# Token blocks turned by four transposing transfers each in the expert stage

## The chip, the core and the metric

The kernel runs on one core of a Trainium2 chip. The core has five engines that work side by side: TensorE (PE: matrix products, with PEld for its weight loads), VectorE (DVE), ScalarE (ACT), GpSimd (POOL) and SyncE (SP, which here only issues DMAs). Each has its own queue of instructions, and they wait for each other on semaphores. Products go to PSUM, which VectorE and ScalarE read; tiles that TensorE reads lie in SBUF. The metric is the time of one execution on the device, in microseconds.

## The reference

One decoder layer on 2 x 1024 tokens of 256 numbers: self-attention with 16 heads, cross-attention with 16 heads over 77 context rows, and a mixture of 8 experts of which each token takes 2, each followed by a residual and a normalisation. The change lies in the experts:

```python
logits = jnp.einsum('bsd,de->bse', x, Wg) + bg
topk_vals, topk_idx = jax.lax.top_k(logits, TOP_K)
topk_w = jax.nn.softmax(topk_vals, axis=-1)
h = jax.nn.relu(jnp.einsum('bsd,edf->bsef', x, W1) + b1)
eo = jnp.einsum('bsef,efd->bsed', h, W2) + b2
sel = jnp.take_along_axis(eo, topk_idx[..., None], axis=2)
mixed = jnp.sum(sel * topk_w[..., None], axis=2)
y = mixed + x
```

## The kernel before

Self-attention fills the first two thirds of the time, cross-attention follows, and the expert stage runs from about 670 us to the end. It computes only the chosen experts. For each half h of the tokens POOL scatters every token's row twice, once for each chosen expert, into a table in memory, `xs[h]` (x_sorted), sorted by expert and padded so that each block of P = 128 rows belongs to one expert. A row has 512 bf16 numbers: 256 that hold the upper part of x and 256 that hold the rest (high and low part). There are HB = 23 blocks a half, BLOCKS = 46 in all. `tab` tells the expert of each block; each engine that needs the number reads it from SBUF into a register (`value_load`: L755 on TensorE, L1358 on ScalarE).

A block m goes through these steps:

- SyncE loads its 128 rows of 1 KB into `xb[:, m % 8]` (`load_block`, L379).
- TensorE turns them (`turn_block`, L748): four transposes of 128 x 128 into a PSUM bank, since the products need the 256 features on the partitions.
- ScalarE copies the bank to `xbT[:, m % 3]` (`keep_block`, L1353).
- TensorE makes the hidden layer (`hidden`, L767): 24 products of 128 x 128 x 128, transposed, with w1 of the expert.
- ScalarE adds the bias and takes the relu (`relu`, L1363, four instructions), VectorE splits the result into a high and a low part (L1036, L1038).
- TensorE makes the output (`output`, L783): 12 products with 256 columns. VectorE adds the bias (`keep_y`, L1049) into one of YB = 3 buffers, and SyncE stores it to `ys[h]` (`store_block`, L384).

When all blocks of a half are stored, POOL gathers two rows for each token (`gather`, L1544), 16 indirect DMAs a half, and VectorE mixes and normalises them. POOL's scatter is L1533, 16 indirect DMAs a half too; the second half's runs beside the first blocks, the first half's gather beside the blocks after the 23rd.

Nothing plans the order: it is the program order of each engine. TensorE's loop over m is turn(m + 3), hidden(m + 2), output(m), with turns 0 to 2 and hidden 0 and 1 ahead of the loop; so in its last three rounds nothing is turned. SyncE has LEAD = 6 loads ahead of the loop, then load(m + 6) and store(m) in each round; a load waits until TensorE has turned the block whose place it takes (`xb_turned`, XB = 8 places).

Of the kernel before, what the change touches and what calls it, by code (L numbers as in the profile page):

```python
# [6 lines left out]
ACT = mybir.ActivationFunctionType  # L7
AX_X = mybir.AxisListType.X
F32 = mybir.dt.float32
BF16 = mybir.dt.bfloat16  # L10
# [3 lines left out]
P = 128  # L14
B, S, D = 2, 1024, 256
# [3 lines left out]
NT = B * S // P  # L19
# [47 lines left out]
XB, YB = 8, 3  # L67
# [3 lines left out]
def build(nc, t):  # L71

    with ExitStack() as ctx:
        def sb(name, shape, dt=F32):
            return ctx.enter_context(nc.sbuf_tensor(name, shape, dt))

        def sem(name):
            return ctx.enter_context(nc.semaphore(name))

        bank = [ctx.enter_context(nc.psum_tensor(f"bank{i}", [P, 512], F32)) for i in range(4, 8)]  # L80
        quad = ctx.enter_context(nc.psum_tensor("quad", [P, 4, 512], F32))
        bank = [quad[:, i, :] for i in range(4)] + [b[:, :] for b in bank]
# [4 lines left out]
        xs = [nc.dram_tensor(f"x_sorted{h}", (XROWS, 2 * D), BF16, kind="Internal").ap() for h in range(2)]  # L87
# [4 lines left out]
        ident16 = sb("ident16", [P, P], BF16)  # L92
# [101 lines left out]
        logits = sb2("logits", [P, NT, NE])  # L194
        second.close()

        xb = sb("xb", [P, XB, 2 * D], BF16)
        xbT = sb("xbT", [P, 3, 4, P], BF16)
        hid = sb("hid", [P, 2, FC, P])
        hh = sb("hh", [P, 2, FC, P], BF16)  # L200
        hl = sb("hl", [P, 2, FC, P], BF16)
# [26 lines left out]
        s2_summed, s2_recip, p2_done, p2_turned, pT_done = map(sem, ("s2_summed", "s2_recip", "p2_done", "p2_turned", "pT_done"))  # L228
# [14 lines left out]
        xb_loaded = [sem(f"xb_loaded{i}") for i in range(XB)]  # L243
        xb_turned, xbT_done = sem("xb_turned"), sem("xbT_done")
        h_ready, hid_done, hh_done, hl_done = map(sem, ("h_ready", "hid_done", "hh_done", "hl_done"))
# [22 lines left out]
        BLOCKS = 2 * HB  # L268
# [10 lines left out]
        def _(sp):  # L279
# [93 lines left out]
            def load_block(m):  # L373
                h, i = m // HB, m % HB
                if i == 0:
                    sp.wait_ge(scattered[h], 16 * 2 * HT)
                if m >= XB:
                    sp.wait_ge(xb_turned, m - XB + 1)
                sp.dma_start(xb[:, m % XB, :], xs[h][i * P:(i + 1) * P, :]).then_inc(xb_loaded[m % XB], 16)  # L379

            def store_block(m):
                h, i = m // HB, m % HB
# [15 lines left out]
            for m in range(LEAD):  # L398
                load_block(m)
# [13 lines left out]
        def _(pe):  # L413
# [75 lines left out]
            for half in range(2):  # L489
                for c in range(C2):  # L490
                    mm = pe.matmul(bank[6][:, half * B * SC:(half + 1) * B * SC], w_in["cwk"][:, c, half * P:half * P + P], ctxT[:, c, :],
                                   start=(c == 0), stop=(c == C2 - 1))
            mm.then_inc(cross_ready, 1)
            for b in range(B):
                for c in range(C2):
                    mm = pe.matmul(bank[7][0:SC, b * D:(b + 1) * D], ctxT[:, c, b * SC:(b + 1) * SC], w_in["cwv"][:, c, :],
                                   start=(c == 0), stop=(c == C2 - 1))
# [94 lines left out]
            def turn_x2(g):  # L592

                pe.wait_ge(x2_done, g * 4 + 4)
                if g:
                    pe.wait_ge(x2T_done, g * 2)
                else:
                    pe.wait_ge(y2_done, 4 * (TG - 1))
                for c in range(C2):
                    for i in range(4):  # L600
                        tr = pe.transpose(bank[6 + c][:, i * P:i * P + P], xres[:, 4 * g + i, c * P:c * P + P], ident[:, :])
                    tr.then_inc(x2_turned, 1)

            def logits2(g):

                pe.wait_ge(x2T_done, 2 * g + 2)
                pe.wait_ge(s2_taken, NT)
                for i in range(4):
                    for c in range(C2):
                        mm = pe.matmul(LOGITS[g][:, i * NE:(i + 1) * NE], x2T[:, c, i * P:(i + 1) * P], wg[:, c, :],  # L610
                                       start=(c == 0), stop=(c == C2 - 1))
                mm.then_inc(logits_ready, 1)
# [99 lines left out]
            for n in range(NT):  # L712
                g, i = n // 4, n % 4
# [23 lines left out]
                    project_o2(g)  # L737


            def turn_block(m):  # L740

                pe.wait_ge(xb_loaded[m % XB], 16 * (m // XB) + 16)
                if m >= 2:
                    pe.wait_ge(xbT_done, m - 1)
                else:
                    pe.wait_ge(pT_done, 3 * NT)
                for c in range(4):
                    tr = pe.transpose(bank[4 + m % 2].bitcast(BF16)[:, c * P:(c + 1) * P], xb[:, m % XB, c * P:(c + 1) * P], ident16[:, :])  # L748
                tr.then_inc(xb_turned, 1)

            def hidden(m):

                h, i = m // HB, m % HB
                pe.wait_ge(tab_done, h + 1)
                e = pe.value_load(tab[0:1, h, i:i + 1], min_val=0, max_val=NE - 1)  # L755
                if m == 0:
                    pe.wait_ge(w_loaded_all, 32)
                    pe.wait_ge(s2_taken, NT)
                pe.wait_ge(xbT_done, m + 1)
                if m >= 3:  # L760
                    pe.wait_ge(hid_done, FC * (m - 2))
                else:
                    pe.wait_ge(logits_taken, m + 1)
                for fc in range(FC):
                    terms = [(half, part, c) for c in range(C2) for half, part in ((0, 0), (0, 1), (1, 0))]
                    for k, (half, part, c) in enumerate(terms):
                        mm = pe.matmul(bank[m % 3][:, fc * P:(fc + 1) * P], w1[:, bass.ds(e, 1), half, c, fc * P:(fc + 1) * P].rearrange("p o f -> p (o f)"),  # L767
                                       xbT[:, m % 3, 2 * part + c, :], start=(k == 0), stop=(k == len(terms) - 1))
                mm.then_inc(h_ready, 1)
                return e  # L770

            def output(m, e):

                pe.wait_ge(hl_done, m + 1)
                if m >= 2:
                    pe.wait_ge(y_done, m - 1)
                elif m == 1:
                    pe.wait_ge(x2T_done, C2 * TG)
                else:
                    pe.wait_ge(y2_done, NT)  # L780
                terms = [(a, half, fc) for fc in range(FC) for a, half in ((hh, 0), (hl, 0), (hh, 1))]
                for k, (a, half, fc) in enumerate(terms):
                    mm = pe.matmul(bank[Y_BANK[m % 2]][:, 0:D], a[:, m % 2, fc, :],  # L783
                                   w2[:, bass.ds(e, 1), half, fc, :].rearrange("p o d -> p (o d)"), start=(k == 0), stop=(k == len(terms) - 1))
                mm.then_inc(y_ready, 1)

            for m in range(3):
                turn_block(m)
            experts = [hidden(0), hidden(1)]
            for m in range(BLOCKS):  # L790
                if m + 3 < BLOCKS:
                    turn_block(m + 3)
                if m + 2 < BLOCKS:
                    experts.append(hidden(m + 2))
                output(m, experts.pop(0))
                if m == 0:
                    pe.wait_ge(y_done, 1)
                    turn_x2(TG - 1)
                    logits2(TG - 1)
                elif m == 1:  # L800
                    rank(2)
                elif m == 2:
                    rank(3)
# [409 lines left out]
        def _(act):  # L1213
# [122 lines left out]
            for n in range(NT):  # L1336
                g, i = n // 4, n % 4
# [8 lines left out]
                    exp2(n + FAR - 1)  # L1346


            def keep_block(m):
                act.wait_ge(xb_turned, m + 1)  # L1350
                if m >= 3:
                    act.wait_ge(h_ready, m - 2)
                act.activation(xbT[:, m % 3, :, :], bank[4 + m % 2].bitcast(BF16)[:, 0:4 * P].rearrange("p (c q) -> p c q", q=P), ACT.Copy).then_inc(xbT_done, 1)  # L1353

            def relu(m):
                h, i = m // HB, m % HB
                act.wait_ge(tab_done, h + 1)
                e = act.value_load(tab[0:1, h, i:i + 1], min_val=0, max_val=NE - 1)  # L1358
                if m >= 2:
                    act.wait_ge(hl_done, m - 1)  # L1360
                act.wait_ge(h_ready, m + 1)
                for fc in range(FC):
                    act.activation(hid[:, m % 2, fc, :], bank[m % 3][:, fc * P:(fc + 1) * P], ACT.Relu, bias=b1[:, bass.ds(e, 1), fc]).then_inc(hid_done, 1)  # L1363

            def exp_gap(h):
                act.wait_ge(gap_done, h + 1)
                act.activation(gw[:, HT * h:HT * h + HT, 1], gw[:, HT * h:HT * h + HT, 0], ACT.Exp).then_inc(gap_exp, 1)
# [4 lines left out]
                    act.activation(acc[:, n, :], acc[:, n, :], ACT.Identity, bias=lnv[:, 6, n:n + 1], scale=lnv[:, 2, n:n + 1]).then_inc(out_done, 1)  # L1372

            exp_gap(0)
            for m in range(3):
                keep_block(m)
            for m in range(BLOCKS):
                relu(m)
                if m == 1:
                    keep_x2(TG - 1)  # L1380
                if m + 3 < BLOCKS:
                    keep_block(m + 3)
                if m == 4:
                    exp_gap(1)
                for g in range(2):
                    if m == LAST[g]:
                        finish_tiles(g)
# [247 lines left out]
```

## Time and profile before

| what | us |
|---|---|
| median of 3 runs | 975.97 (975.21 to 976.09) |
| the profiled execution | 975.68 |
| its span, first to last instruction | 973.9 |
| TensorE busy in the span | 778.8 (80%) |
| VectorE busy | 622.5 (64%) |
| ScalarE busy | 458.0 (47%) |
| POOL busy | 304.3 (31%) |
| mean granted clock of TensorE | 0.905 of 2.4 GHz |

The median is what counts; the profile is one execution, and its times are from the span's start. An engine's busy time tells little by itself: what matters is the chain of waits, which is followed back from the last instruction to whatever released each step. "Issue" in it is time in which an engine waited for nothing that the profile shows. Busy matmuls overlap: one takes 0.2 us from start to end, but the next can start after 0.05 to 0.11 us, so their starts show the pace.

### The profile page before, as it was taken

The numbers are of one execution on the slowest core, as the hardware profiler recorded it, in microseconds if no ns is written. First come the engines' busy times: TensorE is split into PE (matmuls) and PEld (weight loads), VectorE is DVE, ScalarE is ACT, GpSimd is POOL, SyncE is SP. The second block draws the span as 40 slices with busy tenths as digits, with TensorE's granted clock in tenths as the row PEclk, the third lists the DMA queues.
The fourth block names the chain that finished last, engine by engine and source line by source line (L and its number), as shares of the span: only waits on it lengthen the run. The fifth ranks groups of instructions, "written<-read, shape, count | busy, mean of one in ns | idle before, by whom it ended". The sixth has DMA issues, their size and how long they took to land.

```text
span 973.9 us, 14837 instructions
## 1 busy us (share of the span) xinstructions
PE 778.8 (80%) x4736; PEld 384.1 (39%) x4736; DVE 622.5 (64%) x983; ACT 458.0 (47%) x919; POOL 304.3 (31%) x311
## 2 busy tenths in 40 slices
PE   6767999989999999999788887865485998599700
PEld 3433222222222222222235555562364776377600
DVE  3468787877888888888469889652242332286346
ACT  2112667767777777777654324330132443245300
POOL 6000086866000000000146566413323002355074
PEclk9978999999999999999999999957696999599955
DMA  7661529796405040400008000002222222322231
GB/s 223 158 174 52 143 97 273 265 260 220 88 1 88 2 87 2 87 1 1 0 1 345 1 0 1 1 0 91 78 77 87 67 66 83 92 66 62 88 87 43
DMA packets 53682, 86.64 MB, mean 89 GB/s; under 512 B 16425, under 2 KB 41257, under 8 KB 52457
## 3 DMA queue, kind: packets, MB, share of 16 engines
q1 hardware_dynamic: 41689, 53.25, 20.2%
q0 software_dynamic: 9280, 31.20, 9.7%
q10 hardware_dynamic: 2640, 1.24, 0.6%
q8 instruction: 43, 0.70, 0.3%
q14 instruction: 30, 0.25, 0.1%
HBM read 48.15 MB, written 33.03 MB: 83 GB/s over the span
## 4 chain that ended last, share of the span: by engine, by line
PE 57%; DVE 18%; issue 8%; DMA 6%; POOL 4%; ACT 4%; SPq 2%; POOLq 0%; DVEq 0%; ACTq 0%
PE quad L767 10%; PE bank L473 10%; PE bank L481 10%; PE quad L456 8%; PE bank L783 7%; DVE rowmax L838 6%; PE bank L580 3%; DMA qstack<-negrows 2%; PE quad L550 2%; POOL yg L1544 2%; DVE sc L939 1%; DVE xres L913 1%; ACT probs L1257 1%; DMA kstack<-k_parts 1%; PE quad L610 1%
## 5 line engine op out<-in xcount | busy, mean ns | idle before, releaser
L838 DVE TENSOR_REDUCE rowmax<-quad 128x1 f32<-128x1024 f32 x256 | 303.5, 1219 | 75.2 <-PE quad L456 73.8
L1257 ACT ACTIVATE probs<-bank 128x512 f32<-128x512 f32 x512 | 281.8, 595 | 103.7 <-PE bank L473 102.0
L473 PE MATMUL bank<-qstack,kstack 98*128 98x512 bf16 x512 | 193.7, 386 | 17.2 <-ACT probs L1257 9.7
L456 PE MATMUL quad<-kstack,qstack 96*128 96x512 bf16 x512 | 177.2, 386 | 9.3 <-DVE rowmax L838 7.3
L481 PE MATMUL bank<-probs,vslot 128*32 128x512 f32 x1024 | 139.3, 612 | 0.0
L473 PEld LDWEIGHTS bank<-qstack,kstack 98*128 98x128 bf16 x512 | 49.0, 97 | 200.8 <-ACT probs L1257 169.1
L767 PE MATMUL quad<-xbT,w_all 128*128 128x128 bf16 x1104 | 102.8, 232 | 20.9 <-issue 17.3
L767 PEld LDWEIGHTS quad<-xbT,w_all 128*128 x1104 | 79.1, 101 | 43.4 <-issue 29.7
L1353 ACT ACTIVATE xbT<-bank 128x512 bf16<-128x512 bf16 x46 | 27.5, 597 | 146.0 <-PE bank L748 112.7
L1484 POOL TENSOR_TENSOR lnv<-lnv,power 128x4 f32<-128x4 f32 (+1 forms) x8 | 9.6, 1200 | 243.8 <-DVE lnv L891 243.8
L783 PE MATMUL bank<-w_all,hh 128*128 x368 | 72.0, 282 | 10.4 <-issue 8.5
L456 PEld LDWEIGHTS quad<-kstack,qstack 96*128 96x128 bf16 x512 | 48.3, 98 | 72.1 <-DVE rowmax L838 35.0
L1544 POOL DMA_INDIRECT yg<-y_sorted,rowof x32 | 30.8, 961 | 118.4 <-DMA y_sorted<-ysb 109.3
L1036 DVE CAST hh<-hid 128x512 bf16<-128x512 f32 x46 | 21.3, 463 | 63.4 <-ACT hid L1363 63.3
L1049 DVE TENSOR_TENSOR ysb<-bank,b 128x256 f32<-128x256 f32 x46 | 19.5, 425 | 61.0 <-PE bank L783 33.5
L1363 ACT ACTIVATE hid<-quad,b 128x128 f32<-128x128 f32 x184 | 52.7, 368 | 11.3 <-PE quad L767 6.3
L783 PE MATMUL bank<-w_all,hl 128*128 x184 | 51.8, 282 | 4.1 <-issue 4.1
L1533 POOL DMA_INDIRECT x_sorted<-attn,rowof x32 | 31.5, 983 | 66.5 <-DVE rowof L1010 57.3
L1497 POOL TENSOR_TENSOR sc<-sc,max 128x1232 f32<-128x1232 f32 x16 | 36.6, 2290 | 49.2 <-DVE max L944 49.1
L550 PE MATMUL quad<-kbd,q2T 128*128 128x308 f32 x128 | 40.3, 447 | 7.8 <-DVE sc L939 7.8
L783 PEld LDWEIGHTS bank<-w_all,hh 128*128 128x128 bf16 x368 | 36.7, 100 | 23.5 <-issue 15.2
L1502 POOL TENSOR_TENSOR sc<-sc,inv 128x1232 f32<-128x1232 f32 x16 | 35.9, 2251 | 25.8 <-DVE inv L951 25.8
(166 smaller groups left out, 959.2 us busy)
## 6 DMA issues: line engine op xcount, KB each, us to landing
w_all<-w_split SPq DMA_DIRECT2D x2, 4096.0 KB, 18.1
kstack<-k_parts SPq DMA_DIRECT2D x48, 128.0 KB, 7.3
xb<-x_sorted SPq DMA_DIRECT2D x46, 128.0 KB, 2.2
y_sorted<-ysb SPq DMA_DIRECT2D x46, 128.0 KB, 1.7
x_sorted<-zeros POOLq DMA_DIRECT2D x6, 768.0 KB, 8.3
vslot<-v_all SPq DMA_DIRECT2D x8, 512.0 KB, 9.1
w1raw<-in_w POOLq DMA_DIRECT2D x8, 512.0 KB, 5.4
w2raw<-in_w POOLq DMA_DIRECT2D x8, 512.0 KB, 6.3
```

The costliest lines, as they stand in the source:

```text
L456: mm = pe.matmul(bank[2 * (p % 2) + e], q, kstack[slot][0:MAXROW, j, e * 512:e * 512 + 512], start=True, stop=True)
L473: mm = pe.matmul(bank[4 + i % 2], kstack[slot][0:KROWS, j, kt * P:kt * P + P], qstack[slot][0:KROWS, half, j, :], start=True, stop=True)
L481: pe.matmul(bank[6][32 * j:32 * j + VW, :], vslot[slot][:, kt, j, :], probs[:, i % PR, :], start=(kt == 0), stop=(kt == KT - 1), skip_grou ...
L550: mm = pe.matmul(bank[e][:, 0:4 * SC], q2T[:, half, i * P:i * P + P], kbd[:, g // 2, half, 4 * (e % 2):4 * (e % 2) + 4, :].rearrange("p h ...
L767: mm = pe.matmul(bank[m % 3][:, fc * P:(fc + 1) * P], w1[:, bass.ds(e, 1), half, c, fc * P:(fc + 1) * P].rearrange("p o f -> p (o f)"), xb ...
L783: mm = pe.matmul(bank[Y_BANK[m % 2]][:, 0:D], a[:, m % 2, fc, :], w2[:, bass.ds(e, 1), half, fc, :].rearrange("p o d -> p (o d)"), start=( ...
L838: dve.tensor_reduce(rowmax[:, k % 2, p:p + 1], quad[:, 2 * (p % 2):2 * (p % 2) + 2, :].rearrange("p a n -> p (a n)"), AX_X, ALU.max).then_ ...
L1257: act.activation(probs[:, i % PR, :], bank[4 + i % 2], ACT.Exp, scale=INV4).then_inc(probs_ready, 1)
L1363: act.activation(hid[:, m % 2, fc, :], bank[m % 3][:, fc * P:(fc + 1) * P], ACT.Relu, bias=b1[:, bass.ds(e, 1), fc]).then_inc(hid_done, 1)
L1497: pool.tensor_tensor(sc, sc, over_heads(max2[:, n % SR, :]), ALU.subtract).then_inc(s2_shifted, 1)
L1502: pool.tensor_tensor(sc, sc, over_heads(inv2[:, n % SR, :]), ALU.mult).then_inc(p2_done, 1)
L1544: pool.indirect_dma_start(yg[:, i, j, :], None, ys[h], bass.IndirectOffsetOnAxis(ap=rowof[:, j, n:n + 1], axis=0)).then_inc(yg_loaded[i], 16)
```

## The change

The rows of a block are loaded by four transposing DMAs of 128 x 128 each, straight into `xbT`, which now has 8 places in place of 3. `xb`, the transposes on TensorE with their PSUM banks, and the copies on ScalarE are gone. TensorE's `hidden` waits for the loads themselves (four increments of 16 a block), and a load waits, from the ninth block on, until the hidden products of the block in its place are done (`h_ready`).

```diff
-        xb = sb("xb", [P, XB, 2 * D], BF16)
-        xbT = sb("xbT", [P, 3, 4, P], BF16)
+        xbT = sb("xbT", [P, XB, 4, P], BF16)
...
                 if m >= XB:
-                    sp.wait_ge(xb_turned, m - XB + 1)
-                sp.dma_start(xb[:, m % XB, :], xs[h][i * P:(i + 1) * P, :]).then_inc(xb_loaded[m % XB], 16)
+                    sp.wait_ge(h_ready, m - XB + 1)
+                for c in range(4):
+                    sp.dma_start(xbT[:, m % XB, c, :], xs[h][i * P:(i + 1) * P, c * P:(c + 1) * P], transpose=True).then_inc(xb_loaded[m % XB], 16)
...
-            def turn_block(m):
...
-                for c in range(4):
-                    tr = pe.transpose(bank[4 + m % 2].bitcast(BF16)[:, c * P:(c + 1) * P], xb[:, m % XB, c * P:(c + 1) * P], ident16[:, :])
-                tr.then_inc(xb_turned, 1)
...
-                pe.wait_ge(xbT_done, m + 1)
+                pe.wait_ge(xb_loaded[m % XB], 64 * (m // XB) + 64)
...
-                                       xbT[:, m % 3, 2 * part + c, :], start=(k == 0), stop=(k == len(terms) - 1))
+                                       xbT[:, m % XB, 2 * part + c, :], start=(k == 0), stop=(k == len(terms) - 1))
...
-            for m in range(3):
-                turn_block(m)
             experts = [hidden(0), hidden(1)]
             for m in range(BLOCKS):
-                if m + 3 < BLOCKS:
-                    turn_block(m + 3)
...
-            def keep_block(m):
-                act.wait_ge(xb_turned, m + 1)
-                if m >= 3:
-                    act.wait_ge(h_ready, m - 2)
-                act.activation(xbT[:, m % 3, :, :], bank[4 + m % 2].bitcast(BF16)[:, 0:4 * P].rearrange("p (c q) -> p c q", q=P), ACT.Copy).then_inc(xbT_done, 1)
```

TensorE's queue between the output of one block and the hidden layer of block 7, in the fifth round of the loop; `w_all` are the experts' weights and `bank` and `quad` are PSUM. Before:

```order
L783 MATMUL bank<-w_all,hh 128x256
L748 MATMUL bank<-ident,xb 128x128 [waits xbT_done,xb_loaded0]
L748 MATMUL bank<-ident,xb 128x128 x3
L755 TENSOR_LOAD tab [waits tab_done]
L755 ISA x2
L767 ISA [waits hid_done,xbT_done]
L767 MATMUL quad<-xbT,w_all 128x128 x2
```

And now:

```order
L772 MATMUL bank<-w_all,hh 128x256
L744 TENSOR_LOAD tab [waits tab_done]
L744 ISA x2
L756 ISA [waits hid_done,xb_loaded7]
L756 MATMUL quad<-xbT,w_all 128x128 x2
```

The register load follows the output's products directly, and the hidden products wait for the DMAs of their own block.

SyncE's queue from the first load of a block on. Before:

```order
L379 DMA xb<-x_sorted 128x512 [waits scattered0]
L379 DMA xb<-x_sorted 128x512 x6
L384 DMA y_sorted<-ysb 128x256 [waits y_done]
L379 DMA xb<-x_sorted 128x512
L384 DMA y_sorted<-ysb 128x256 [waits y_done]
L379 DMA xb<-x_sorted 128x512 [waits xb_turned]
```

And now:

```order
L379 DMA_TRANSPOSE xbT<-x_sorted 128x128 [waits scattered0]
L379 DMA_TRANSPOSE xbT<-x_sorted 128x128 x27
L384 DMA y_sorted<-ysb 128x256 [waits y_done]
L379 DMA_TRANSPOSE xbT<-x_sorted 128x128 x4
L384 DMA y_sorted<-ysb 128x256 [waits y_done]
L379 DMA_TRANSPOSE xbT<-x_sorted 128x128 [waits h_ready]
L379 DMA_TRANSPOSE xbT<-x_sorted 128x128 x3
```

Each load has become four, and each store of y stands behind four of them in place of one; 28 stand ahead of the first store.

## Rows read from the trace of the kernel before

**Rows 1.** Page, part 4: chain that ended last, by line
```profile
PE quad L767 10%; PE bank L473 10%; PE bank L481 10%; PE quad L456 8%; PE bank L783 7%; DVE rowmax L838 6%; PE bank L580 3%; DMA qstack<-negrows 2%; PE quad L550 2%; POOL yg L1544 2%; DVE sc L939 1%; DVE xres L913 1%; ACT probs L1257 1%; DMA kstack<-k_parts 1%; PE quad L610 1%
```

**Rows 2.** Windows: us; PE, PEld, DVE, ACT, POOL busy (instructions); clock; DMA; GB/s
```profile
745.00:825.00 80.00, 76.80 (x794) 61.58 (x792) 30.67 (x61) 34.17 (x99) 3.92 (x5) 0.98 0.24 73
...
726.00:744.00 18.00, 5.06 (x30) 2.22 (x28) 0.00 (x0) 0.00 (x0) 11.97 (x13) 0.65 0.24 95
825.00:843.00 18.00, 4.81 (x17) 1.53 (x17) 1.54 (x3) 1.74 (x5) 11.53 (x12) 0.55 0.38 110
```

**Rows 3.** Chain of waits, 776 to 793: start, us, what
```profile
776.51 1.46 PE bank L783 x12
777.97 0.22 PE bank L748 x4
778.19 0.26 issue
778.46 2.21 PE quad L767 x24
780.67 1.46 PE bank L783 x12
...
782.52 2.18 PE quad L767 x24
784.69 1.46 PE bank L783 x12
...
786.48 2.27 PE quad L767 x24
788.76 1.46 PE bank L783 x12
...
790.64 2.23 PE quad L767 x24
792.87 1.46 PE bank L783 x12
```

**Rows 4.** Timeline of the same stretch: start, us, engine, line, operation, tiles
```profile
776.62 0.69 DVE L1038 TENSOR_TENSOR hl<-hid,hh 128x512 bf16<-128x512 f32 x1
...
777.81 0.39 PE L748 MATMUL bank<-ident,xb 128*128 128x128 bf16 x4
```

**Rows 5.** TensorE's register load (L755), two blocks: ns min/median/max, first, last start
```profile
L755 PEldq TENSOR_LOAD <-tab x1: 306/306/306, 777.4 to 777.4; - x1
...
L755 PEldq TENSOR_LOAD <-tab x1: 299/299/299, 913.3 to 913.3; - x1
```

**Rows 6.** Chain of waits, the last blocks, which turn nothing between
```profile
912.46 1.46 PE bank L783 x12
...
914.19 2.18 PE quad L767 x24
```

**Rows 7.** Chain of waits where VectorE is on it
```profile
870.02 0.70 DVE hl L1038
```

**Rows 8.** Tile xbT, all its instructions: who waited for it (us, times)
```profile
  PE quad L767: 0.6, 1
```

**Rows 9.** Chain of waits at the first block
```profile
696.18 2.74 PE quad L767 x24
```

**Rows 10.** Timeline of SyncE's queue (SPq), at the start and in a full stretch
```profile
691.21 3.17 SPq L379 DMA_DIRECT2D xb<-x_sorted  x7
...
778.57 0.32 SPq L384 DMA_DIRECT2D y_sorted<-ysb  x1
778.93 1.42 SPq L379 DMA_DIRECT2D xb<-x_sorted  x1
```

**Rows 11.** Line 379, all 46 loads: ns min/median/max of the issue, us to landing
```profile
L379 SPq DMA_DIRECT2D xb<-x_sorted x46: 320/432/1873, 691.2 to 899.5; - x46
...
DMA to landing us min/median/max: 2.1/2.2/3.8
```

**Rows 12.** DMA queues from 750 to 770: packets, MB, share of 16 engines
```profile
q1 hardware_dynamic: 1440, 1.31, 21.6%
```

More of the change, by code:

```diff
@@ L737, in _ @@
                     project_o2(g)
-            def turn_block(m):
[L742 to L746, printed above, removed]
-                for c in range(4):
-                    tr = pe.transpose(bank[4 + m % 2].bitcast(BF16)[:, c * P:(c + 1) * P], xb[:, m % XB, c * P:(c + 1) * P], ident16[:, :])
-                tr.then_inc(xb_turned, 1)
             def hidden(m):
@@ L1374, in _ @@
             exp_gap(0)
-            for m in range(3):
-                keep_block(m)
             for m in range(BLOCKS):
@@ L1380, in _ @@
                     keep_x2(TG - 1)
-                if m + 3 < BLOCKS:
-                    keep_block(m + 3)
                 if m == 4:
```

## The prediction

> **What bounds the kernel now.** I read the chain of waits first, by line [rows 1]. The lines of this change, L767 (hidden products, 10% of the span) and L783 (output products, 7%), are TensorE's, and the transposes (L748) don't reach the list. The change can only work from 691 us, where the first block is loaded, to some 920 us, where the last product ends. The windows say how full TensorE is there [rows 2]: 76.80 of 80 us at clock 0.98 from 745 to 825. Two stretches are otherwise: 726 to 744 has 5.06 of 18 us, with no work on VectorE or ScalarE and 13 indirect DMAs on POOL, and 825 to 843 looks alike. There TensorE's instructions come slowly while POOL scatters or gathers, so POOL ends such a stretch, not the blocks' work. In the full stretches the chain goes only over TensorE, block by block [rows 3]: L783 for 1.46 us, four transposes for 0.22, "issue" for 0.26, L767 for about 2.2. Four periods from 776.51 to 792.87 make 4.09 us a block.
>
> **TensorE's part: what the four transposes really cost.** The plain count: the four together take 0.39 us from 777.81 and the next hidden product starts at 778.46 [rows 3, 4]. That is 0.65 us from the first transpose on; at 0.43 (four slots of 0.11, some 1.3 us over the 12 products of L783) 43 blocks would give 18 us. But the chain has "issue" behind the transposes: TensorE could not start L767 yet. What it waits for is its own sequencer, which reads the expert's number (L755). That load starts at 777.4, before the first transpose runs, and L767 follows 1.0 us later [rows 5]. The trace has one place that shows the loop without transposes: the last three blocks turn nothing, so the output at 912.46 is followed by L767 directly, at 914.19 [rows 6]. That is 1.73 us from output start to hidden start. With transposes between, the four pairs of [rows 3] take 1.95, 1.85, 1.79 and 1.88, mean 1.87. The load of the number starts 0.9 us after the output's start in both (777.4, 913.3), and L767 0.9 to 1.0 us after it [rows 5]. So the transposes mostly lie in the shade of the register load, and when they go, "issue" takes their place: the gain is 0.14 us a block. Its bounds are 0.06 (1.79 less 1.73) and 0.22 (1.95 less 1.73).
>
> How many blocks get it: 43 of the 46 turns lie inside the loop. Two fall into POOL's stretches, where the end is POOL's; two more blocks wait for VectorE anyway (an hl at 870.02, [rows 7], and one like it at 878.88). 39 times 0.14 is **5.5 us**, with 2.3 and 8.6 from the bounds.
>
> **ScalarE's part.** 46 copies go. ScalarE had 34.17 us of work in 80 [rows 2], and L767 waited for the copy 0.6 us in the whole trace [rows 8]: nothing. The hand-over of the hidden layer does not become the next limit either: hl is there at 777.31 (776.62 + 0.69, [rows 4]) and the output that reads it starts at 780.67, 3.4 us of slack that become 3.2.
>
> **The start.** Now 691.21 (first load issued) to 696.18 (first L767) [rows 9, 10]: the load of block 0, of 1 and 2, the transposes, the copy, TensorE's register load. After: four issues, the landing, then L767, the number read long before. Seven issues took 3.17 us, 0.45 each, and a load landed in 2.2 us [rows 10, 11]: 691.2 + 1.8 + 2.2 = 695.2, 1.0 earlier; with the 1.42 us issue of [rows 10] and the longest landing of 3.8 it would be 700.7, 4.5 later. I take a gain of **0.7 us**.
>
> **SyncE's part, the new work.** One load of 128 KB becomes four transposing ones of 32 KB: 184 for 46 loads, all on SyncE's queue, each iteration's four standing ahead of the store of y, for which VectorE's third-next y and POOL's gather wait. The trace has no transposing transfer, so I bound it by the nearest rows. Issue: a plain load holds the queue 0.43 us, 0.32 at least; slow ones took 1.42 and, the longest, 1.87 [rows 10, 11]. Per block 4 x 0.43 + 0.36 for the store (778.57 to 778.93) is 2.1 us of the 3.95 us that a block would last: hidden. Transfer: 1440 hardware packets took 21.6% of 16 engines for 20 us, 48 ns each, and the engines idle most of each block [rows 12]. The same bytes in rows of 256 B are 512 packets, 1.5 us on 16 engines, with the store 1.9: hidden. It is loaded six blocks (over 20 us) ahead, so latency is hidden too. I take nothing; the nearest row is the same load in plain form.
>
> From where this cover is gone: the last of the 184 must land before the last hidden block. That started at 914.2; less 2.2 us of landing it is 912.0. From 691.2 this leaves 220.8 us, less 39 stores of 0.36 (14.0) it is 206.8, and over 184 **1.12 us each, for no change**. To keep the whole gain (6.2 us) it must be under 1.09. One number for the whole stage will do, as SyncE goes on loading while TensorE stands in POOL's stretches. The same price holds for a transfer that can't overlap the next.
>
> Here the Trainium skill speaks against the change. Its page "VectorE: DVE Perf Modes", section "The three transpose paths", gives 1309 ns for a 128x128 bf16 transpose by DMA against 390 ns on TensorE. The trace has no row for the first; for the second it has 0.39 us for all four [rows 4], so the page's figures seem to be those of one operation alone. Were 1.309 us what each costs in a row, the estimate would be 691.2 + 240.9 + 14.0 + 2.2 = 948.3, 34 us later than 914.2, and about 1010 us in all. On the other side, "Advanced Engine Details and Errata", section "X-Bar Transpose (TRN2)", says that transposing DMAs are as fast as regular ones; no row here shows it, and by it nothing would be lost.
>
> **Sum.** 5.5 + 0.7 = 6.2 us off the profiled execution's 975.68 (span 973.9) is 969.5; the median of the runs is 0.3 higher, so **969.8 us**. Its own range is 966 to 974.
>
> **Rivals.**
> 1. *The queue or the transposing transfers become the bound* (slower). Mechanism: each of the 184 holds SyncE's queue, or the DMA engines one after another, longer than 1.12 us; TensorE then waits at L756 for each block, and the period is 4 times that price plus 0.36. For it: such a transfer is a different instruction, must write 2-byte elements over 128 partitions, and even plain issues reach 1.87. Against it: the median of 0.43. At 1.42 each: 184 x 1.42 = 261 and 691.2 + 261.3 + 14.0 + 2.2 = 968.7, 54.5 late, 1030 us; at 1.12 976; at 1.87 it would be 1113. TensorE's clock may fall in the gaps, as it does to 0.65 in 726 to 744; the first L767, after 20 us of idle TensorE, took 2.74 us for 2.2 [rows 9], so even a slower block (some 4.6 us by that ratio) fits into the 6.0 us of such a period. Chance 0.40; the page's figure lies inside it.
> 2. *The gain is nothing* (same). The cost per transfer lies near 1.1 us, or the transposes were hidden altogether (1.79 against 1.73), or the start is a few us late: 974 to 978. Chance 0.10.
> 3. *The transposes' whole time comes back*, because the sequencer reads the number earlier: 39 x 0.43 = 17, and 958 us. For it: the sequencer runs ahead of TensorE by some matmuls. Against it: in [rows 6] it did not. Chance 0.03.
>
> **Chances.** The forecast 0.47, and 1, 2 and 3 as given. A measurement tells 0.2%, 2 us, from no change. Most of the forecast, rival 3 and a bit of rival 2 are faster: 0.47. Within 0.2%: 0.11. Slower: 0.42. The range 964 to 1030 reaches over rival 2 and rival 1 up to 1.42 us.
>
> **What would show it.** Right: SyncE's issues of L379 at about 0.45 to 0.55 us; no DMA in front of L756; 1.73 us from an output's start to the next hidden product; first L756 at 695 to 696; the period 3.95. Wrong: L379 over 1.1 us each with TensorE waiting for DMA xbT, its clock falling; landings that grow from block to block; or "issue" in front of L756 smaller than 0.2 us, which would be rival 3. The part that I trust least is the price of one transposing transfer.

## The result and the profile after

| what | before | after |
|---|---|---|
| median, us (4 runs each) | 975.97 (975.21 to 976.09) | 1020.44 (1018.37 to 1022.55) |
| ratio | | 1.046, 95% interval 1.043 to 1.048 |
| the profiled execution, us | 975.68 | 1018.37 |
| its span | 973.9 | 1016.5 |
| TensorE busy | 778.8 (80%) | 771.7 (76%) |
| ScalarE busy | 458.0 (47%) | 430.8 (42%) |
| mean granted clock of TensorE | 0.905 | 0.893 |

The change makes the kernel 4.6% slower. The work did leave TensorE and ScalarE. A new name stands in the chain of waits: SyncE's queue. The chain that ended last, by engine and the head of the list by line (its counterpart before is [rows 1], where L767 and L783 held 17% of the span):

```profile
PE 40%; DVE 20%; SPq 17%; issue 8%; DMA 6%; POOL 5%; ACT 3%; POOLq 0%; DVEq 0%; ACTq 0%
```

The by-line list begins with SPq L379 at 14%; L756 and L772, the hidden and output products, have 2% each. The instructions of L379, with their issue times (ns, minimum, median, maximum) and landing, answer to [rows 11]:

```profile
L379 SPq DMA_TRANSPOSE xbT<-x_sorted x184: 961/1232/2646, 685.3 to 953.4; - x184
...
DMA to landing us min/median/max: 2.2/2.3/4.2
```

A transposing transfer holds SyncE's queue for 1.23 us, where a plain one held it for 0.43. The transfer itself lands 2.3 us after the start of its issue, as the plain one did (2.2); the trace has the landing of 48 of the 184. TensorE's waits for loads of blocks (us, times, longest), before and after:

```profile
PE bank L748 <- DMA xb<-x_sorted: 22.6, 2, 22.2
PE quad L756 <- DMA xbT<-x_sorted: 74.4, 26, 26.6
```

The longest of each is the wait for the very first block, which both kernels have. Without it TensorE waited 0.4 us before and 47.8 us, in 25 waits, now. The hidden products' only wait before was 0.6 us for ScalarE's copy [rows 8].

The store of y stands behind four of these in the same queue. Its line, with who waited for it:

```profile
L384 SPq DMA_DIRECT2D y_sorted<-ysb x46: 320/578/2079, 722.5 to 964.4; - x46
...
  DVE ysb L1034: 104.9, 25
```

It now takes 0.58 us in place of 0.32 [rows 10]. VectorE, which needs one of the three y buffers back, waited for it 25 times. SyncE's queue in a stretch without POOL's transfers (start, us, what; compare [rows 10]):

```profile
777.02 0.58 SPq L384 DMA_DIRECT2D y_sorted<-ysb  x1
777.64 4.92 SPq L379 DMA_TRANSPOSE xbT<-x_sorted  x4
782.60 0.58 SPq L384 DMA_DIRECT2D y_sorted<-ysb  x1
783.23 4.92 SPq L379 DMA_TRANSPOSE xbT<-x_sorted  x4
```

The queue is not idle: 0.58 + 4.92, with 0.04 to 0.05 between one issue and the next, make a period of 5.6 us a block, where TensorE needed 4.09 [rows 3]. In the whole stage, from the first to the last issue of L379, the longest gap between two of its issues is 0.40 us: the queue never stops. In this stretch the chain of waits is nothing else, piece after piece (from 727 to 760 and from 858 to 925 it goes over TensorE and VectorE, beside POOL's work, while the queue issues on):

```profile
799.93 0.58 SPq L384
800.51 0.04 issue
800.55 1.10 SPq L379
801.65 0.04 issue
801.70 1.23 SPq L379
```

What that does to the engines stands in the windows (columns as in [rows 2]), then the DMA queue's packets, megabytes and share of 16 engines:

```profile
775.00:800.00 25.00, 16.33 (x151) 12.45 (x148) 5.80 (x12) 5.17 (x19) 0.00 (x0) 0.93 0.17 45
800.00:825.00 25.00, 16.39 (x144) 13.09 (x144) 5.80 (x12) 4.58 (x16) 0.00 (x0) 0.86 0.17 45
```

And the DMA queue between 775 and 800:

```profile
q1 hardware_dynamic: 3296, 1.08, 16.4%
```

TensorE is busy 65% of the time where it was busy 96% [rows 2], and its granted clock falls from 0.98 to 0.93 and 0.86, as means over stretches in which it changes between its two levels (2.4 and 1.2 GHz). The transfer engines carry more and smaller packets than before [rows 12] and are still idle five sixths of the time.

**Where the 42.7 us between the two profiled executions went.** The first load is issued at 685.25 in place of 691.21: stages that the diff doesn't touch ran 6.0 us faster in this execution. From there to the landing before the last hidden block (953.37 + 2.40, 955.8) it is 270.5 us; before, from 691.21 to 914.19 [rows 6, 10], it was 223.0. That is 47.5 more. What follows is 1.1 longer. Together 47.5 + 1.1 - 6.0 = 42.6. The stage is an account of SyncE's queue. By its single records 183 issues of L379 with a mean of 1.27 us and 39 stores with a mean of 0.65 lie between 685.3 and 953.4, each with a gap of 0.046: 183 x 1.32 + 39 x 0.69 = 268.5, where 268.1 was measured. The means stand over the medians (1.23, 0.58) because of long ones: 15 issues of L379 took over 1.4 us, 12 us more together than at the median.

### The profile page after: what moved, and what is told of

The parts are those of the page before. It is cut to its first block, busy times and chain, and to the rows that moved or that the text cites. A ratio compares the mean times of both kernels' runs of the same rounds, so it can differ in the third digit from the quotient of the medians.

```text
span 1016.5 us, 14472 instructions
## 1 busy us (share of the span) xinstructions
PE 771.7 (76%) x4552; PEld 379.4 (37%) x4552; DVE 621.5 (61%) x983; ACT 430.8 (42%) x873; POOL 303.6 (30%) x311
## 4 chain that ended last, share of the span: by engine, by line
PE 40%; DVE 20%; SPq 17%; issue 8%; DMA 6%; POOL 5%; ACT 3%; POOLq 0%; DVEq 0%; ACTq 0%
SPq L379 14%; PE bank L473 9%; PE bank L481 9%; PE quad L456 8%; DVE rowmax L823 6%; PE bank L772 2%; DMA qstack<-negrows 2%; PE quad L756 2%; PE bank L580 2%; PE quad L550 2%; DVE sc L924 2%; POOL yg L1519 2%; DVE max L929 1%; DVE xres L898 1%; ACT probs L1242 1%
## 5 line engine op out<-in xcount | busy, mean ns | idle before, releaser
L756 PE MATMUL quad<-xbT,w_all 128*128 128x128 bf16 x1104 | 105.5, 248 | 88.9 <-DMA xbT<-x_sorted 74.4
L756 PEld LDWEIGHTS quad<-xbT,w_all 128*128 x1104 | 86.1, 109 | 112.8 <-issue 101.8
L772 PE MATMUL bank<-w_all,hh 128*128 x368 | 78.3, 297 | 18.8 <-DVE hl L1023 9.3
L772 PE MATMUL bank<-w_all,hl 128*128 x184 | 54.8, 298 | 4.8 <-issue 4.8
L772 PEld LDWEIGHTS bank<-w_all,hh 128*128 128x128 bf16 x368 | 39.3, 107 | 30.7 <-issue 21.5
L427 PE MATMUL bank<-xT,wqkv 128*128 128x512 f32 x64 | 33.4, 660 | 7.4 <-DMA xT<-in_xT 7.3
L1260 ACT ACTIVATE pT<-bank 128x512 f32<-128x512 f32 (+1 forms) x48 | 23.6, 525 | 35.3 <-PE bank L565 35.2
## 6 DMA issues: line engine op xcount, KB each, us to landing
w_all<-w_split SPq DMA_DIRECT2D x2, 4096.0 KB, 17.6
```

## Experiments

The theory after the result (A): each transposing DMA holds SyncE's queue about 1.23 us, whatever its size, and that queue sets the pace. Rival theories: (B) the time is each 128 x 128 piece's, wherever it is issued from; (C) the transfers or the DMA engines are the limit and hold the queue back; (D) something else of the change costs it, such as the new wait, four semaphore increments, or strided rows. The chips differ: the kernel before takes 941.8, 943.1, 972.2 and 973.8 us on the four used here, so only ratios to it on the same chip, or kernels of one chip, are compared. The expectations give times for a kernel before of 976 us, unless they say otherwise; the ratio is what to compare.

**One transposing DMA for each block.** Edit of the changed kernel (TensorE's wait is adapted, 16 per block):

```diff
-                for c in range(4):
-                    sp.dma_start(xbT[:, m % XB, c, :], xs[h][i * P:(i + 1) * P, c * P:(c + 1) * P], transpose=True).then_inc(xb_loaded[m % XB], 16)
+                sp.dma_start(xbT[:, m % XB, :, :], xs[h][i * P:(i + 1) * P, :], transpose=True).then_inc(xb_loaded[m % XB], 16)
```

> The changed kernel, but one transposing transfer of 128x512 a block in place of four of 128x128 (same bytes, same result). Theory A, the queue pays per instruction: an issue stays near 1.23 us, SyncE has 46 of them, about 1.9 us a block with the store, hidden; L756 waits for nothing and the time is about 970 us. Theory B, the queue pays per piece of a transfer: one issue takes about 4.5 to 4.9 us and the time stays at 1015 to 1020. Theory C, the transfer itself is the bound: the issue is short but the landing grows to 5 us and more and TensorE waits for it, 1010 to 1020.

Measured: 936.51 us against 941.83, ratio 0.9947 (0.9927 to 0.9967). Its issues and landing, and SyncE's queue:

```profile
L378 SPq DMA_TRANSPOSE xbT<-x_sorted x46: 1194/1196/2399, 688.5 to 858.9; - x46
...
DMA to landing us min/median/max: 2.5/2.7/4.4
```

SyncE's queue, from the timeline:

```profile
765.47 0.32 SPq L383 DMA_DIRECT2D y_sorted<-ysb  x1
765.83 1.19 SPq L378 DMA_TRANSPOSE xbT<-x_sorted  x1
```

Four times the bytes in one instruction take 1.20 us to issue, no more than 32 KB did, and land 0.4 us later. B and C fall: the same bytes are turned and moved, and TensorE waits for no block but the first, for which it waits in every version. SyncE's issues take 1.5 of 3.9 us; the issue is 1.20 us long although the queue had stood idle for 2.4 us before the store ahead of it, so it isn't a backlog of earlier transfers that holds it. This version does what the change meant to do, and is faster than both kernels.

**The same, on another chip.** The edit is that of the run before.

> The kernel with one transposing DMA of 128 x 512 per block a second time, beside the kernel before on the same chip, with nothing left out of the computation. It gave a ratio of 0.9947 [0.9927, 0.9967] on a chip where the kernel before takes 941.8 us. If the gain is TensorE's (about 0.12 us in each full block, transposes that no longer stand behind the output products), it stays at 3 to 7 us whatever chip it runs on: a ratio of 0.993 to 0.997. If it came from something particular to that chip, such as how the blocks fall against POOL's indirect DMAs, the ratio may be 1.000 or above. The issue of each transposing DMA should again take 1.2 us.

Measured: 966.99 us against 973.81, ratio 0.9943 (0.9922 to 0.9963), issue 1.195 us. The gain of 5 to 7 us holds on a chip on which the kernel before takes 32 us longer.

**Four plain DMAs, and one.** First only `transpose=True` goes; then also the loop over c, as above. Nothing turns the blocks in these two, so TensorE multiplies unturned rows; the number and size of the transfers are those of the changed kernel and of the version with one transposing DMA.

```diff
-                    sp.dma_start(xbT[:, m % XB, c, :], xs[h][i * P:(i + 1) * P, c * P:(c + 1) * P], transpose=True).then_inc(xb_loaded[m % XB], 16)
+                    sp.dma_start(xbT[:, m % XB, c, :], xs[h][i * P:(i + 1) * P, c * P:(c + 1) * P]).then_inc(xb_loaded[m % XB], 16)
```

> The changed kernel with its four transfers of 128x128 a block made plain; the turning is left out, so the blocks that TensorE reads are not turned. If it is the transposing that makes an issue long, L379 falls to about 0.43 us each, a block costs SyncE 2.1 us and the time is 968 to 972. If the number of transfers or their 256 B rows make it, the time stays well over 976.

> The changed kernel with one plain transfer of 128x512 a block, again without any turning: the change's effect on TensorE and ScalarE alone, with SyncE as before. The forecast of the prediction for that part was 0.14 us a block and 0.7 at the start: 969 to 971. The rival, the transposes' whole time back: about 958. If the transposes were hidden altogether: 974 to 976.

Measured: four plain ones 935.63 us, 0.9943 (0.9921 to 0.9965); one plain one 935.91 us, 0.9922 (0.9899 to 0.9946). The issues of the four, SyncE's queue beside them, and last the chain of waits with one:

```profile
L379 SPq DMA_DIRECT2D xbT<-x_sorted x184: 319/432/1606, 690.0 to 862.9; - x184
```

Their timeline:

```profile
760.34 0.32 SPq L384 DMA_DIRECT2D y_sorted<-ysb  x1
760.71 1.89 SPq L379 DMA_DIRECT2D xbT<-x_sorted  x4
```

The chain of waits with one plain DMA:

```profile
756.96 1.46 PE bank L771 x12
758.41 0.33 issue
758.74 2.18 PE quad L755 x24
760.92 1.46 PE bank L771 x12
...
762.58 2.27 PE quad L755 x24
```

D falls: with the same waits, increments and strided rows, 184 issues cost 0.43 us each, and four with their gaps 1.9, which is hidden. It is the turning alone that makes an issue 1.23. From output start to hidden start it is now 1.78 and 1.66 us, against a mean of 1.87 before [rows 3], and "issue" fills what the transposes left. By the single records of all blocks from 745 to 820 the median is 1.70 us in this run, in the one with four plain DMAs and in the one with one transposing DMA, and 1.83 in both profiles of the kernel before: 0.13 a block.

**Two of the four transposing.** The two pieces of the high part are turned, those of the low part are loaded plain, and so its products read unturned rows.

```diff
-                    ...c * P:(c + 1) * P], transpose=True).then_inc(xb_loaded[m % XB], 16)
+                    ...c * P:(c + 1) * P], transpose=c < 2).then_inc(xb_loaded[m % XB], 16)
```

> The changed kernel with two of the four transfers of a block transposing and two plain (the low part of x is left unturned). By the price per issue SyncE needs 2 x 1.27 + 2 x 0.43 + 0.6 = 4.0 us a block, at the 3.95 of TensorE: 968 to 978. If a transposing transfer held up what comes behind it in the DMA engines, more than 985.

Measured: 951.15 us, ratio 1.0108 (1.0061 to 1.0154). That is slower than I had put it (0.992 to 1.002), and as slow as I had put it for the other case, a transposing transfer that holds up what comes behind it (over 1.009). The two kinds of issue, SyncE's queue, and VectorE's wait for the store:

```profile
L379 SPq DMA_TRANSPOSE xbT<-x_sorted x92: 1094/1227/2685, 689.7 to 883.6; - x92
L379 SPq DMA_DIRECT2D xbT<-x_sorted x92: 343/573/1486, 692.3 to 885.5; - x92
```

From the timeline:

```profile
764.61 0.44 SPq L384 DMA_DIRECT2D y_sorted<-ysb  x1
765.10 2.37 SPq L379 DMA_TRANSPOSE xbT<-x_sorted  x2
```

From VectorE's waits (us, times, longest):

```profile
DVE ysb L1034 <- DMA y_sorted<-ysb: 51.3, 20, 4.4
```

The count by instruction holds (92 of 1.23), but I had not counted that a plain issue right behind a transposing one costs more as well: by the single records the third issue of a block takes 0.58 us and the fourth, behind a plain one, 0.43. So something is held up, but it is seen in the queue: the stores still land after 1.8 us (1.7 in the version with one transposing DMA). The trace has no landing of the loads. With the medians and gaps the queue has 4.0 us of work a block, with the long issues (the means) 4.4, more than TensorE's 3.94. From the first issue to the last it is 195.8 us, with no gap over 0.40 us: SyncE's queue sets the pace here too, and the time needs no further cause. TensorE waited 11.4 us for blocks behind the first, in 11 waits.

**The changed kernel again, and with the stores of y on ScalarE's queue.** The first is unedited, to have it on the chip of the second. In the second each store stands three blocks late in ScalarE's queue, behind a relu.

```diff
             for m in range(BLOCKS):
                 relu(m)
+                if m >= 3:
+                    store_block(m - 3)
...
+            for m in range(BLOCKS - 3, BLOCKS):
+                store_block(m)
```

> The changed kernel once more, unedited, beside the others. The chip of the first four experiments has no stretches in which TensorE's instructions come slowly beside POOL's indirect DMAs (before takes 942 us there, not 976). If SyncE's queue sets the pace of the whole stage, such stretches were absorbed in the changed kernel and their absence gives it little: 1005 to 1020 where before takes 942 (ratio 1.07 to 1.08), and 1020 where before takes 976. If the loss were a fixed addition to TensorE's time, the ratio would be 1.046 to 1.048 again, 986 where before takes 942.

> The changed kernel with the 46 stores of y issued from ScalarE's queue in place of SyncE's. Theory A, the queue's time: SyncE's period falls from 4 x 1.27 + 0.62 = 5.7 to 5.1 us, and 40 blocks give back 23 to 25 us against the changed kernel. Theory C, the transposing transfers or the engines behind the queue: within 5 us of the changed kernel.

Measured, with the kernel before at 943.1: the changed kernel 1020.24 us, ratio 1.082 (1.076 to 1.088); with the stores elsewhere 1001.75, ratio 1.061 (1.054 to 1.067). The issues of L379, the unedited kernel first, and the stores in the second:

```profile
L379 SPq DMA_TRANSPOSE xbT<-x_sorted x184: 1093/1232/2668, 688.3 to 955.9; - x184
```

With the stores on ScalarE's queue:

```profile
L379 SPq DMA_TRANSPOSE xbT<-x_sorted x184: 1093/1234/2324, 689.7 to 936.8; - x184
...
L1350 ACTq DMA_DIRECT2D y_sorted<-ysb x46: 326/334/379, 718.0 to 947.1; - x46
```

The first of these says the most. The kernel before is 33 us faster on this chip than on the first, and the changed kernel isn't faster at all: its 184 issues take 267.6 us here and took 268.1 there. What bounds it is the queue, and the queue is alike on both. In the second the queue holds nothing but L379: the issuing spans 247.1 us, 20.5 less, and the time falls by 18.5, not by the 23 to 25 that I had expected. The single records tell why. The first transposing issue behind a store takes 1.10 us (800.55 above), and without stores it is 1.23 like the others; the mean issue went from 1.27 to 1.30. A store in this queue thus costs 0.5 us net, not 0.62. On ScalarE's queue, where nothing transposing stands, a plain store is issued in 0.33 us.

**What the four transposes cost where nothing hides them.** TensorE reads the number of the first block's expert once and uses it for all blocks, so that neither the register load nor the arithmetic for the weights' addresses is left in the loop. The hidden and output products use one fixed expert, in the same number and size; the register operations ahead of the hidden products fall from 736 to 16. Both on the kernel before and on the version with one plain load (part of the edit):

```diff
-                e = pe.value_load(tab[0:1, h, i:i + 1], min_val=0, max_val=NE - 1)
+                e = first[0] if first else pe.value_load(tab[0:1, h, i:i + 1], min_val=0, max_val=NE - 1)
+                first.append(e)
```

> The kernel before, with its transposes on TensorE, and the same leaving out of register load and address arithmetic on TensorE. The pair with the run before it tells what the transposes cost when nothing hides them: if they lay in the shade of the register load, the difference between the two is 10 to 18 us (0.22 to 0.43 us a block), where with the loads it was 6. If the transposes cost the same in both, 6 us again.

> One plain transfer a block (nothing is turned) and, on TensorE, the first block's expert for all blocks: the register load and with it all address arithmetic of TensorE is left out. If TensorE's sequencer sets the pace of the hidden products and of the gap before them, the period falls from 3.94 to about 2.8 us (24 x 0.056 + 12 x 0.109 + 0.1), some 45 us less than with the loads. If TensorE itself does, nothing changes.

Measured: before, without load 908.11 us, ratio 0.9617 (0.9557 to 0.9677); one plain load, without register load 900.6, ratio 0.9548 (0.9483 to 0.9612). The chains of waits, with the transposes and without:

```profile
756.43 0.22 PE bank L748 x4
756.65 1.34 PE quad L770 x24
757.99 1.31 PE bank L786 x12
759.30 0.22 PE bank L748 x4
```

Without the transposes:

```profile
755.63 1.34 PE quad L758 x24
756.97 1.31 PE bank L774 x12
758.28 1.34 PE quad L758 x24
```

A block lasts 2.87 us with and 2.65 without, so four unhidden transposes cost 0.22 us, 0.056 each, and not the 0.43 of the plain count. By the single records of 22 blocks from 745 to 820 it is 1.53 against 1.31 from output start to hidden start, 0.22 again, where the versions with the register load differ by 0.13. The whole time does not show that: the two medians differ by 7.5 us, where I had expected 10 to 18, and with intervals of 6 us on each this is no more than the 6 us that I had put for "the same in both". The pair also shows what the work of TensorE's sequencer costs: 24 hidden products take 1.34 us in place of 2.2, and the kernel before gets 35 us faster without it. The version with one plain load gains as much by its ratios (0.9922 and 0.9548), where I had expected 45.

**A version meant to be better still: hidden and output products mixed.** If the sequencer holds up the hidden products, those of block m + 2 may go 2 to 1 between the output products of block m. Done on the version with one transposing load, and on the kernel before.

```diff
...
+                for _ in range(3 * FC):
+                    take(outs, 1)
+                    take(hids, 2)
...
```

> One transposing transfer a block, and TensorE's program interleaves block m+2's hidden products with block m's output products (two and one in turn), same work and result. The leaving out of address arithmetic took 35 us off, so TensorE's sequencer sets the pace of the hidden products (0.085 us each) and TensorE itself that of the outputs (0.109). If the two limits alternate, the mixture overlaps them: a block falls from 3.94 to 3.3 to 3.6 us and the time by 15 to 25 us against the unmixed kernel of 936 (ratio to before 0.967 to 0.978). If the sequencer is the bound all the time, no change: ratio 0.994.

> The same interleaving in the kernel before, which keeps its transposes on TensorE. It tells whether the transposing transfer is worth something once the interleaving is there: the transposes take 4 x 0.056 = 0.22 us of TensorE a block or less, so 5 to 10 us above the interleaved kernel with transposing transfers; the same time if the sequencer hides them.

> The kernel before, unedited, for its profile on the chip of the other runs: about 942 us, a period of 4.07 us a block as in the first profile, and no stretches of slow instructions on TensorE beside POOL's indirect DMAs.

Measured, with the kernel before at 972.2: 985.26 us, ratio 1.0145 (1.009 to 1.020), and 995.65, ratio 1.0244 (1.019 to 1.030). Both are slower than before; for the first I had expected 0.967 to 0.978, or 0.994. The second lies 10.4 us above the first, at the upper end of the 5 to 10 that I had put. The kernel before, profiled on this chip, misses its expectation too: 972.98 us in one run, with the slow stretches beside POOL's indirect DMAs, since this was not the chip of the runs before. The windows from 850 to 900, the mixed one first and then the kernel before, with TensorE's waits for VectorE in them (us, times, longest):

```profile
850.00:900.00 50.00, 31.34 (x304) 26.16 (x305) 33.22 (x73) 11.97 (x40) 24.12 (x58) 0.80 0.17 43
```

TensorE waiting for VectorE in it:

```profile
PE bank L773 <- DVE hl L1044: 15.7, 4, 4.9
```

The kernel before, in the same windows:

```profile
850.00:900.00 50.00, 46.25 (x478) 36.63 (x476) 38.20 (x84) 24.25 (x68) 26.57 (x58) 1.00 0.21 64
```

And the kernel before's waits:

```profile
PE bank L783 <- DVE hl L1038: 1.4, 2, 0.8
```

There VectorE mixes the tokens of the first half beside the blocks. In the usual order an output stands behind 2.2 us of hidden products, and a late hl is hidden by them; mixed, the first output product stands at the block's start, and TensorE waited 15.7 us in place of 1.4, with its clock at 0.80. From one read of the expert's number to the next four blocks there take 6.4, 8.9, 8.9 and 8.3 us, where the longest of the unmixed version (on the chip of 973.8) take 4.1, 4.8, 4.9 and 4.4: 14 of the 18 us between the two versions' medians. In the full stretches nothing is won either. The start of the last output product of one block and of the first hidden product of the next:

```profile
774.68 0.27 PE L773 MATMUL bank<-w_all,hh 128*128 x1
775.56 0.28 PE L756 MATMUL quad<-xbT,w_all 128*128 128x128 bf16 x2 [0.61 <-ACT hid L1363]
```

The 36 products between take 3.1 us, where 3.4 of the unmixed version's 3.94 are products, but the gap is 0.9 in place of 0.5, and the period from 771.62 to 775.56 is 3.94, as without mixing. The row blames ScalarE; since the register load stands in the same gap, the trace does not tell which of the two sets its length, and no run was made for it.

## Why the prediction was wrong

The forecast was 969.8 us and faster. It is 1020.4 and slower: rival 1 came true, near the upper end of the stated range (964 to 1030).

**SyncE's part failed.** The step is "the nearest row is the same load in plain form": I took 0.43 us for an issue whose kind the trace did not have. The break-even of 1.12 was the number to judge by, and the issue takes 1.23 by the median and 1.32 with gap and long ones. The edit from four plain to four transposing DMAs, with nothing else changed, shows that the kind of instruction is all of it (0.43 against 1.23). The plain rows of 1.42 and 1.87, from which rival 1 took its bounds, did not point to it either: they are long ones of any kind, and the transposing issues have their own, up to 2.65. That the range holds the result is in part luck, since 1.42 happens to lie close to 1.32. No row before could tell the price, so the median of another kind of instruction was a choice, not a measurement. The mechanism that rival 1 described, TensorE waiting at L756 with a period of four issues and a store, is what the profile shows; its chance was 0.40 and, with no row for this kind of instruction, should not have been below the forecast's.

The Trainium skill's page "VectorE: DVE Perf Modes", section "The three transpose paths", gives 1309 ns for a 128x128 bf16 transpose by DMA. That page of the Trainium skill does not say which part of the transfer this is. In this kernel the issue comes near it, with 1.23 us and 1.32 a piece in a row, and the landing (2.3) does not; it was the only price of this very operation that I had. It is not a price by size here: 128 x 512 took 1.20 us. The Trainium skill's page "Advanced Engine Details and Errata", section "X-Bar Transpose (TRN2)", says that transposing DMAs are as fast as regular ones. The trace agrees for the landing (2.3 against 2.2 us) and not for the issue (1.23 against 0.43), which that sentence does not mention; the measurement decides.

**The store's price was too low too.** The sum by rival 1 took 0.36 for a store, and it is 0.69 behind transposing issues with gap and long ones, 13 us more over 39. With 1.32 for the load and 0.36 for the store the rival's own sum is 691.2 + 242.9 + 14.0 + 2.2 = 950.3; with 13 more for the stores and 6.0 less for the earlier start it gives 957, and 955.8 was measured; most of the rest is that the landing counts from the start of the last issue, so that 183 issues lie before it and not 184. What follows the last hidden block came out 1.1 us longer, for which I had no term.

**TensorE's part was right.** I had 5.5 us, 0.14 a block; the medians of 1.83 and 1.70 us give 0.13. It rested on one place without turning (1.73), and such places range from 1.67 to 1.87 in the full stretches of the versions without transposes, so that it lay so near their median was luck. The version with one transposing DMA gains 5.3 and 6.8 us on two chips, and the one with a plain DMA 5.9 us by the medians and 7.3 by its ratio; the start has a share in these (below). In the changed kernel itself, at a place without a wait, output start to hidden start is 1.80 and 1.73 us (the prediction's 1.73 without turning):

```profile
752.42 1.47 PE bank L772 x12
753.89 0.32 issue
754.22 2.22 PE quad L756 x24
756.44 1.46 PE bank L772 x12
...
758.17 1.86 PE quad L756 x20
```

"Issue" took the transposes' place, as I had said, so rival 3 is out. What was off is the plain count against which I argued: the four transposes' true price is 0.22 us, of which 0.13 showed.

**ScalarE's part and the transfers.** As forecast: the 27 us less of work on ScalarE give nothing by themselves, since TensorE hardly waited for that copy, and the transfer engines are 16% busy. **The start** is not told by the result, as the stages ahead of it moved too. From the first issue to the first hidden product it is 6.5 us (685.25 to 691.8) in place of 5.0 [rows 9, 10]: 1.5 us worse where I had 0.7 better, since four issues at 1.27 take 5.1 us and not 1.8. With one transposing DMA a block it is 3.5 us (688.46 to 691.98), 1.5 better. **The clock** fell to 0.93 and 0.86, as rival 1 had it, and cost nothing that shows, since SyncE's queue had no gaps in which it waited for TensorE.

## What to carry to other kernels

Count the instructions that a queue must issue, not only the bytes: a queue that issues for a loop is an engine with a period of its own, and a kind of instruction that the trace does not have must be priced from a measurement of that kind, not from its plain relative. If a transposing DMA is to take the place of TensorE's transposes, make it as large as the block (one issue of 1.20 us in place of four of 1.23); the same idea was 4.6% slower in four pieces and 0.5% faster in one. Removing an operation gives back only the time in which nothing else would have held up its engine: 0.13 of 0.22 us here, as the read of the expert's number lay beside it.

## What the hardware showed that I had not expected

- A transposing DMA takes 1.20 us to issue for 128 x 512 and 1.23 for 128 x 128, where a plain one takes 0.43 (both median). The landing is 2.7 and 2.3 us.
- A plain issue right behind a transposing one in the same queue takes 0.58 us, otherwise 0.32 to 0.43. In the version with one transposing DMA, where the queue stood idle between the two, the store took 0.32.
- Products whose weights' address TensorE's sequencer works out anew for each block start every 0.09 us (24 in 2.2 us); the same products without this register arithmetic start every 0.056 us (24 in 1.34).
- The kernel before takes 942, 943, 972 and 974 us on four chips, and took 976 where the result was measured. In the profiles from the slower ones TensorE's instructions come slowly beside POOL's indirect DMAs, and in those from the faster ones they don't. The windows from 725 to 745 in the version with one transposing DMA, on the chip where the kernel before takes 942 and on that where it takes 974:

```profile
725.00:745.00 20.00, 18.56 (x185) 14.13 (x183) 7.35 (x15) 5.98 (x22) 9.36 (x10) 1.00 0.43 135
```

The same kernel on the slower chip:

```profile
725.00:745.00 20.00, 8.51 (x68) 6.31 (x68) 3.80 (x11) 3.42 (x12) 8.55 (x9) 0.57 0.26 92
```

The work there is the same. On the slower chip two blocks of this version last 19.3 and 17.6 us, on the faster one none after the first few over 4.9 (from one read of the expert's number to the next), and these two make up 29 of the 30.5 us between the medians. Why the chips differ was not found.
